# High and low halves interleaved element by element in a four-layer graph network kernel

## The reference

```python
# layer 0
Wh = h @ W0;  e = leaky_relu(Wh @ a[:512] + (Wh @ a[512:]).T, 0.2)
att = softmax(where(adj > 0.5, e, -9e15), axis=1);  x += elu(att @ Wh)
# layer 1
Ah = adj + I;  d = rsqrt(sum(Ah, -1))
x += relu((d[:, None] * Ah * d[None, :]) @ h @ K1 + bias)
# layer 2
x += relu((adj @ h) @ K2) * (any(h != 0, -1))
# layer 3
agg = adj @ h / max(sum(adj, -1), 1e-6);  x += relu(concat([h, agg], -1) @ W3.T)
```

## Time and profile before

| | |
|---|---|
| median of 3 executions | 2623.15 us |
| profiled execution, its own time | 2621.74 us |
| its span | 2619.9 us |
| mean granted TensorE clock | 0.992 |
| instructions | 40393 |

### The profile page before, as it was taken

How to read it: one execution, slowest core, us unless ns; L and a number is a source line. 1 busy time by engine, 2 the same in 40 slices (tenths; PEclk the granted TensorE clock), 3 DMA queues, 4 the chain that set the end, 5 groups by cost and what they waited for, 6 DMA issues and landing times.

```text
span 2619.9 us, 40393 instructions
## 1 busy us (share of the span) xinstructions
PE 2547.1 (97%) x13704; PEld 2205.5 (84%) x13704; DVE 1823.2 (70%) x4251; ACT 1408.7 (54%) x2571; POOL 1185.2 (45%) x1607
## 2 busy tenths in 40 slices
PE   2799999999999999999999999999999999999998
PEld 2688888888888888888888888888888888888886
DVE  6776676676676677677677777777776766766753
ACT  3555555555555555555555555555555555555542
POOL 2544444444444444444444444444444444444431
PEclk8899999999999999999999999999999999999999
DMA  4101111111011011011111111111111111111000
GB/s 140 41 29 49 33 41 49 33 41 49 30 44 49 29 45 49 29 45 46 33 45 41 37 45 41 37 45 35 42 46 33 41 49 33 41 49 33 29 17 25
DMA packets 72844, 109.30 MB, mean 42 GB/s; under 512 B 4288, under 2 KB 37056, under 8 KB 72640
## 3 DMA queue, kind: packets, MB, share of 16 engines
q1 hardware_dynamic: 72640, 106.71, 12.6%
HBM read 73.14 MB, written 33.55 MB: 41 GB/s over the span
## 4 chain that ended last, share of the span: by engine, by line
PE 96%; DVE 1%; issue 1%; ACT 1%; POOL 1%; DMA 0%; SPq 0%; POOLq 0%; ACTq 0%; DVEq 0%
PE O L277 46%; PE T L277 34%; PE X L277 13%; PE X L310 2%; PE X L298 1%; POOL h_lo L747 0%; ACT h L405 0%; DMA act_out<-w_all 0%; POOL xs L712 0%; DVE p_lo L589 0%; DVE scores L522 0%; DVE w_lo L512 0%; DVE t_lo L595 0%; ACT act_out L436 0%; DVE xs L630 0%
## 5 line engine op out<-in xcount | busy, mean ns | idle before, releaser
L747 POOL TENSOR_TENSOR h_lo<-h,h_hi 128x512 fp32r<-128x512 f32 x384 | 503.4, 1333 | 673.1 <-ACT h_hi L411 673.1
L595 DVE TENSOR_TENSOR t_lo<-T,t_hi 128x512 fp32r<-128x512 f32 x512 | 352.5, 690 | 399.1 <-ACT t_hi L417 399.1
L405 ACT ACTIVATE h<-xs,ln_bias,ln_scale 128x512 f32<-128x512 f32 x512 | 396.0, 811 | 391.9 <-POOL ln_bias L741 391.9
L277 PE MATMUL O<-w_hi,t_hi 128*128 128x512 f32 x1536 | 603.2, 393 | 0.0
L277 PE MATMUL O<-w_hi,t_lo 128*128 128x512 f32 x1536 | 598.2, 389 | 0.0
L277 PE MATMUL O<-w_lo,t_hi 128*128 128x512 f32 x1536 | 598.1, 389 | 0.0
L417 ACT CAST t_hi<-T 128x512 fp32r<-128x512 f32 x512 | 298.3, 584 | 257.1 <-PE T L277 257.1
L712 POOL TENSOR_TENSOR xs<-xs,act_out 128x512 f32<-128x512 f32 x128 | 163.7, 1297 | 531.7 <-ACT act_out L439 496.9
L277 PEld LDWEIGHTS O<-w_hi,t_lo 128*128 128x128 f32 x1536 | 288.3, 188 | 60.2
L277 PEld LDWEIGHTS O<-w_hi,t_hi 128*128 128x128 f32 x1536 | 288.5, 188 | 55.9 <-DVE t_lo L595 0.5
L277 PEld LDWEIGHTS O<-w_lo,t_hi 128*128 128x128 f32 x1536 | 288.6, 188 | 55.7
(11 more groups left out here) (92 smaller groups left out, 4991.4 us busy)
## 6 DMA issues: line engine op xcount, KB each, us to landing
xs<-x SPq DMA_DIRECT2D x64, 512.0 KB, 3.6
out<-xs SPq DMA_DIRECT2D x64, 512.0 KB, 2.8
a_raw<-adj_t SPq DMA_DIRECT2D x64, 256.0 KB, 2.7
a_rows<-adj SPq DMA_DIRECT2D x64, 256.0 KB, 2.7
xs<-w_all SPq DMA_DIRECT2D x6, 512.0 KB, 7.3
act_out<-w_all SPq DMA_DIRECT2D x2, 512.0 KB, 6.7
z<-w_all SPq DMA_DIRECT2D x2, 512.0 KB, 6.4
v_rows<-a_vecs SPq DMA_DIRECT2D x1, 512.0 KB, 5.4
```

The source lines that it names most:

```text
L277: last = nc.tensor.matmul(psum, s, m, start=(start and n == 0 and i == 0), stop=(stop and n == len(pairs) - 1 and i == 2))
L405: nc.scalar.activation(h[:, k.odd, m], xs[:, k.xb, m], ACT.Relu, bias=ln_bias[:, k.quad, m:m + 1], scale=ln_scale[:, k.quad, m:m + 1], acc ...
L595: nc.vector.tensor_tensor(t_lo[:, k.odd, c], T[:, c], t_hi[:, k.odd, c].bitcast(F32), ALU.subtract).then_inc(t_lo_ready, 1)
L747: nc.gpsimd.tensor_tensor(h_lo[:, k.odd, m], h[:, k.odd, m], h_hi[:, k.odd, m].bitcast(F32), ALU.subtract).then_inc(h_lo_ready, 1)
```

## The change

`h`, `t` and transposed `h` are held as one tensor each with a last axis of two, high half and low half side by side; the old names become views with a step of two elements. In layer 3, where `t` is the streamed operand, the same memory is used as two contiguous blocks through the view `u_split`. The padding tensor ahead of `v_rows` grows from 96 to 112 floats (64 bytes), a new one of 112 floats stands behind `a_lo`, and `p_distance` grows from 48 to 64 floats. So `xs`, `a_raw`, `a_hi` and `a_lo` lie 64 bytes further on, `h`, `t` and `ht` begin 512 bytes further on, and `p` 576 bytes.

```diff
-        distance = sb("distance", [P, 96])
+        w_distance = sb("w_distance", [P, 112])
...
+        a_distance = sb("a_distance", [P, 112])
...
-        h_hi = sb("h_hi", [P, 2, NT, F], F32R)
-        h_lo = sb("h_lo", [P, 2, NT, F], F32R)
-        t_hi = sb("t_hi", [P, 2, FT, N], F32R)
-        t_lo = sb("t_lo", [P, 2, FT, N], F32R)
-        ht_hi = sb("ht_hi", [P, FT, N], F32R)
-        ht_lo = sb("ht_lo", [P, FT, N], F32R)
+        h_split = sb("h_split", [P, 2, NT, F, 2], F32R)
+        t_split = sb("t_split", [P, 2, FT, N, 2], F32R)
+        ht_split = sb("ht_split", [P, FT, N, 2], F32R)
+        h_hi, h_lo = h_split[:, :, :, :, 0], h_split[:, :, :, :, 1]
+        t_hi, t_lo = t_split[:, :, :, :, 0], t_split[:, :, :, :, 1]
+        ht_hi, ht_lo = ht_split[:, :, :, 0], ht_split[:, :, :, 1]
+        u_split = t_split[:].rearrange("p b f n s -> p b (f n s)").rearrange("p b (s m n) -> p b s m n", s=2, m=NT)
+        u_hi, u_lo = u_split[:, :, 0], u_split[:, :, 1]
...
-        p_distance = sb("p_distance", [P, 48])
+        p_distance = sb("p_distance", [P, 64])
...
-                        u = slice(HALF * m, HALF * m + HALF)
-                        parts.append((a_hi[:, k.ab, m, c], a_lo[:, k.ab, m, c], flat(t_hi[:, k.odd, u]), flat(t_lo[:, k.odd, u])))
+                        parts.append((a_hi[:, k.ab, m, c], a_lo[:, k.ab, m, c], u_hi[:, k.odd, m], u_lo[:, k.odd, m]))
...
-                nc.scalar.copy(t_hi[:, k.odd, c], T[:, c]).then_inc(t_hi_ready, 1)
+                if k.layer == 3:
+                    nc.scalar.copy(u_hi[:, k.odd, b], flat(T[:, c])).then_inc(t_hi_ready, 1)
+                else:
+                    nc.scalar.copy(t_hi[:, k.odd, c], T[:, c]).then_inc(t_hi_ready, 1)
...
-                nc.vector.tensor_tensor(t_lo[:, k.odd, c], T[:, c], t_hi[:, k.odd, c].bitcast(F32),
-                                        ALU.subtract).then_inc(t_lo_ready, 1)
+                if k.layer == 3:
+                    nc.vector.tensor_tensor(u_lo[:, k.odd, b], flat(T[:, c]), u_hi[:, k.odd, b].bitcast(F32),
+                                            ALU.subtract).then_inc(t_lo_ready, 1)
+                else:
+                    nc.vector.tensor_tensor(t_lo[:, k.odd, c], T[:, c], t_hi[:, k.odd, c].bitcast(F32),
+                                            ALU.subtract).then_inc(t_lo_ready, 1)
```

## The result

The changed kernel takes 2685.66 us (median of 4 runs, 2683.46 to 2686.26) against 2623.09 us for the kernel before on the same chip. The ratio is 1.0242, interval 1.0229 to 1.0255: 62.6 us slower, where 2599 us and at most 2645 were forecast. The profiled execution has a span of 2684.0 us against 2619.9 us, 64.1 us more.

A forecast was written before the change was run, and what follows sets the result against it. TensorE was taken as the bound, its time set by the matmul pitch. Gains of 20.3 + 1.9 + 1.7 = 23.9 us, from a median of 2623.15, gave 2599 us, with a range of 2585 to 2645 us.

The forecast's parts named there:

- What bounds the kernel: TensorE throughout: no other engine is late for it, so only a change of the matmul pitch moves the time much.
- The isolated matmuls: Weight products: two matmuls without a load beside them last 0.39 us like all others, so loads cost nothing; no gain taken.
- Part 1: Gathers with 256 columns: pitch falls from 117.9 to 113.5 ns, 4608 x 4.4 ns = 20.3 us less.
- the equal pace of load and stream: Gathers: spread load and 256-column stream both span 1024 bytes and would stay half of 512 bytes apart.
- The quiet 113.5 ns: Gathers: pitch seen around 138 us after a pause, for the same operands usually at 117.9; taken as the new pitch.
- nothing moves: Rival on the gathers: the 4.4 ns come from how a stage is entered, not layout; about 2623 us, chance 0.16.
- Part 2: Last gather, t streamed against a: distance becomes 256 like the weight products', 768 x 2.5 ns = 1.9 us less.
- Part 3: Weight products settling after transposes: 27 ns in each of 64 places would go, 1.7 us less.
- Part 4: Other engines writing and reading halves at every second element: hidden behind TensorE even at twice the time, 0 taken.
- the spread load disturbs more: Rival on gathers and weight products: 20 us and 41 us more; 2643, 2664 or 2684 us, chance 0.22.

The follow-up runs named there:

- e3: Changed kernel with high and low halves alternating in blocks of 128 elements in place of single ones: 2630.64 us, ratio 1.0032 to the kernel before.
- s1: Separate kernel of matmul lines only, sweeping step and distance of the stationary tile: 226.7 to 233.3 ns for 512 columns at a step of one.
- e7: Changed kernel with t and ht back in tensors of their own, only h interleaved: 2633.24 us against 2621.36 before, ratio 1.0043.
- s2: Second matmul-only sweep, varying tile width, broadcast operands, distance and preceding matmul: narrower tiles 230.0 and 231.7 ns, one streamed broadcast column 218.5 ns.
- e1: Kernel before with only the three paddings changed, high and low halves in tensors of their own: 2629.52 us against 2621.41, ratio 1.0029.
- e5: Kernel before with only paddings changed, to the distances fastest in the sweep: 2621.61 us against 2621.21, ratio 1.0002.
- e4: Changed kernel with h and t halves interleaved four by four, a step of four, ht at two: 3373.47 us, ratio 1.2864 to the kernel before.
- v1: Kernel before with the eight transposes of h moved ahead of the layer-2 gather: 2618.15 us against 2621.36, ratio 0.9986.

## Why the prediction was wrong

**What bounds the kernel** was right: TensorE has no gap before or after, and the 64.1 us of the spans are all pitch.

**The isolated matmuls were read wrongly, and this is the step that let the largest term pass.** From two matmuls of 0.39 us with no load beside them I took that the load costs the weight products nothing, and gave products whose streams keep their layout no price. That term, put at nothing, measured 7.1 ns for each of 7680 products, 54 of the 64 us; e3, s1 and e7 tie it to the step of two in the stationary `t` and `ht`. In the changed kernel the last matmul ahead of a pause looks like this (timeline of PE):

```profile
117.97 0.39 PE L280 MATMUL O<-w_lo,t_split 128*128 128x512 f32 x1
118.20 0.40 PE L280 MATMUL O<-w_hi,t_split 128*128 128x512 f32 x1
122.10 0.36 PE L280 MATMUL T<-p_hi,h_split 128*128 128x256 f32 x1 [3.50 <-issue]
```

Nothing is loaded beside the one at 118.20, and it takes 0.40 us, no less than its neighbours with their pitch of 234. So such a matmul doesn't show whether loads disturb the stream, and the earlier trace rows couldn't bear the conclusion. That the 226.7 ns of contiguous tiles hold little of the load s2 makes likely, but only for the one distance at which they were. The rows that spoke against "the load costs nothing" were on my table: the last gather at 229.2 ns had the same widths and contiguous tiles and differed from the weight products in distance, besides what is streamed. I priced that difference as a gain and didn't ask what it says of the products if their loads change.

**Part 1, the gathers.** Forecast 4608 x 4.4 ns less, measured 2.1 ns more each, 10 us. Two assumptions failed. The distance of 256 bytes was taken for the farthest point of 512; s1 shows that places repeat every 256 bytes, so it is a distance of 0, and for 256 columns the slower one (e1: 2.87 us with contiguous tiles). And the equal pace of load and stream doesn't keep them apart: a step of two is at 120 ns at d = 64 as well as at 256 (L86, L89). The quiet 113.5 ns are a matter of the phase in which a stage is entered, which the rival "nothing moves" had said. They were no price for a layout.

**Part 2, the last gather**, was right where it stands alone: 2.72 us in e1 and e5. In the changed kernel it takes 2.75 us, though e1, e3 and e7 with the same places have 2.72. What differs is the spread product ahead of it, and the last gather has to settle from there (timeline of PE, 1019.3 to 1022.5 us):

```profile
1019.35 0.62 PE L280 MATMUL O<-t_split,a_hi 128*128 128x512 f32 x2
...
1020.74 0.62 PE L280 MATMUL O<-t_split,a_hi 128*128 128x512 f32 x2
...
1022.11 0.28 PE L280 MATMUL T<-a_hi,h_split 128*128 128x256 f32 x1
```

Its first six matmuls take 1.39 us, 232 ns each, and the last six 1.37.

**Part 3** did not come: the products behind the transposes take 5.61 us for 24, no less than those behind other products (5.60).

**Part 4, the other engines**, was right that they stay hidden. Their own price is small: the cast to `t_hi` with a step of two takes 629 ns in place of 584, `h_hi` 1135 in place of 1051, `h_lo` 1355 in place of 1333, `t_lo` 691 in place of 690:

```profile
L422 ACT CAST t_split<-T 128x512 fp32r<-128x512 f32 x384 | 241.1, 629 | 238.4 <-PE T L280 238.4
```

**The rival "the spread load disturbs more"** named the mechanism and the place, the weight products. Its chance of 0.22 was too low and its price for the products too small: 7680 x 5.3 = 41 us against 54 measured, while that for the gathers was too large, 20 us against 10.
## What to carry to other kernels

When TensorE has no gap, the pitch of each stage is the whole kernel; read it from the chain of waits, for each kind of stage apart, and price any change to how a stationary tile lies in memory as a change of that pitch, even where the streams are untouched. Keep each stationary tile of float32 contiguous; if it can't be, keep the step at two and try the place in steps of 64 bytes, which was worth 27 us of 2686 here. A sweep of some hundred microseconds in a kernel of its own gives the table of distances before anything is rebuilt.

## What the hardware showed that I had not expected

- In float32r at the 2.4 GHz level, 512 streamed columns take 226.7 ns where 512 cycles are 213.3; one broadcast column streamed as often takes 218.5 (s2).
- The start of the stationary tile against the start of the stream counts modulo 256 bytes: 226.7 to 233.3 ns for 512 columns, 117.9 to 120 for 256 (s1), where a quiet phase of 113.4 exists too (s2).
- A stationary tile costs 120, 172 and 237 ns per matmul with steps of two, three and four under 256 streamed columns (s1, L89, L96, L97).
- A streamed operand had no free step among the two tried: a step of two takes 453 ns for 512 columns (s1, L99), of four 461 (e4).
- The same gather, at the same addresses, has two settled pitches, 117.9 and 113.4 ns, and the order of the stages can decide which it gets (v1).
